# One fused layer kernel: the experts' results scattered to token order by GpSimd, and read back by plain transfers

## The reference

```
out = x + attention(xn) + experts(xn)
```

```
gate_logits = xn @ gate_w + gate_b                     # 8 experts
top_idx     = top_k(gate_logits, 2)
all_out     = relu(xn @ expert_w[e] + expert_b[e])     # e = 0..7
experts     = mean of all_out over the two chosen e
```

## Time and profile before

| | us |
|---|---|
| time, median of 3 runs | 1613.08 (1612.5 to 1616.36) |
| the profiled execution's own time | 1613.21 |
| its span | 1611.5 |
| TensorE busy | 1512.8 (94%) |
| VectorE busy | 1137.4 (71%) |
| ScalarE busy | 902.2 (56%) |
| GpSimd busy | 583.6 (36%) |
| mean granted clock of TensorE | 0.975 of full |

### The profile page before, as it was taken

How to read it: one execution, slowest core, us unless ns; L and a number is a source line. 1 busy time by engine, 2 the same in 40 slices (tenths; PEclk the granted TensorE clock), 3 DMA queues, 4 the chain that set the end, 5 groups by cost and what they waited for, 6 DMA issues and landing times.

```text
span 1611.5 us, 44000 instructions
## 1 busy us (share of the span) xinstructions
PE 1512.8 (94%) x12544; PEld 809.9 (50%) x12545; DVE 1137.4 (71%) x2384; ACT 902.2 (56%) x1629; POOL 583.6 (36%) x788
## 2 busy tenths in 40 slices
PE   5799989999999999999999999999999899999697
PEld 2788844444444444454444444444444455555233
DVE  5788778887777777777777777777777244444366
ACT  1677746666666666666666666666666433332000
POOL 2444402323454454432232223222322543332653
PEclk9899979999999999999999999999999999999798
DMA  6588851223222322233223322232232466554787
GB/s 161 164 268 271 236 151 52 72 67 93 71 69 62 90 77 70 64 83 84 70 63 81 85 70 63 81 86 70 63 78 63 135 207 217 177 174 142 253 280 250
DMA packets 161456, 198.05 MB, mean 123 GB/s; under 512 B 45792, under 2 KB 95072, under 8 KB 161024
## 3 DMA queue, kind: packets, MB, share of 16 engines
q1 hardware_dynamic: 125088, 117.11, 24.9%
q10 hardware_dynamic: 23328, 44.60, 9.4%
q0 software_dynamic: 12992, 35.77, 7.4%
HBM read 109.13 MB, written 63.12 MB: 107 GB/s over the span
## 4 chain that ended last, share of the span: by engine, by line
PE 79%; DVE 8%; issue 5%; DMA 3%; SPq 2%; ACT 1%; POOL 1%; DVEq 0%; ACTq 0%; POOLq 0%
PE PS L1328 29%; PE PS L1383 28%; PE PS L1433 12%; PE PS L1457 5%; DVE pm L1122 4%; PE PS L1415 2%; DMA arena<-in_x 1%; SPq L423 1%; DVE mx L1127 1%; SPq L415 1%; DVE mx L1126 1%; DVE arena L988 0%; PE PS L1274 0%; DMA q_pieces<-w_hi 0%; DMA arena<-in_Wuv 0%
## 5 line engine op out<-in xcount | busy, mean ns | idle before, releaser
L1122 DVE TENSOR_REDUCE pm<-PS 128x1 f32<-128x512 f32 (+3 forms) x1280 | 717.0, 602 | 200.3 <-PE PS L1328 185.3
L871 ACT ACTIVATE arena<-PS 128x512 f32<-128x512 f32 (+1 forms) x1152 | 613.5, 574 | 300.0 <-PE PS L1328 277.9
L1328 PE MATMUL PS<-arena 97*64 97x512 f16 (+7 forms) x5120 | 693.5, 353 | 26.6 <-DVE pm L1122 20.3
L1383 PE MATMUL PS<-arena 128*33 128x512 f32 (+3 forms) x2560 | 634.7, 531 | 1.9 <-POOL arena L649 1.9
L1328 PEld LDWEIGHTS PS<-arena 96*64 96x64 f16 (+1 forms) x5120 | 329.3, 110 | 416.3 <-DVE pm L1122 140.1
L649 POOL TENSOR_SCALAR_AFFINE_SELECT arena<-arena 128x256 f32<-128x256 f32 (+1 forms) x256 | 111.5, 436 | 546.7 <-ACT arena L871 545.6
L1383 PEld LDWEIGHTS PS<-arena 128*33 128x33 f32 x2560 | 159.4, 111 | 81.5 <-POOL arena L649 2.6
L1433 PE MATMUL PS<-w_hi,arena 128*128 x576 | 172.5, 381 | 0.7 <-issue 0.7
L890 ACT ACTIVATE arena<-PS 128x1024 f16<-128x1024 f32 x72 | 73.8, 1024 | 143.5 <-PE PS L1415 141.4
L1328 PE MATMUL PS<-later,deny 128*64 128x128 f16 x1024 | 145.4, 222 | 0.0
L1186 DVE SCALAR_TENSOR_TENSOR arena<-PS,eb_bc 128x512 f32<-128x512 f32 x72 | 49.8, 692 | 114.8 <-PE PS L1433 111.3
(11 more groups left out here) (174 smaller groups left out, 1296.8 us busy)
## 6 DMA issues: line engine op xcount, KB each, us to landing
expert_rows<-arena SPq DMA_DIRECT2D x72, 256.0 KB
comb_hl<-arena SPq DMA_DIRECT2D x256, 64.0 KB
arena<-q_pieces ACTq DMA_DIRECT2D x90, 128.0 KB
arena<-k_pieces ACTq DMA_DIRECT2D x90, 128.0 KB
v_rows<-w_lo SPq DMA_DIRECT2D x8, 1056.0 KB, 7.5
arena<-in_x SPq DMA_DIRECT2D x16, 512.0 KB, 5.7
xn_rows<-arena SPq DMA_DIRECT2D x16, 512.0 KB, 6.1
q_pieces<-w_hi SPq DMA_DIRECT2D x32, 256.0 KB, 5.3
```

What stands on the lines that cost most here:

```text
L871: a.activation(probs[kk % 4][:, a_ * CH:a_ * CH + w], PS[:, s2_bank(k, x), 0:w], ACT.Exp, scale=SCALE).then_inc(s["exp_done"], 1)
L1122: v.reduce_max(pm[:, c, r, p:p + 1], PS[:, S1_BANK[n], 0:w], AX).then_inc(s["s1_done"], 1)
L1328: last = t.matmul(PS[h:h + P // 2, bank, cols], lhsT[:, h:h + P // 2], rhs, start=start, stop=stop)
L1383: last = t.matmul(PS[rows_, 6 + c % 2, CH - wds[a]:CH], v_sb[pu % 2][:, j + a, :], probs[pk % 4][:, a * off:a * off + wds[a]], start=p_ in ...
```

## The change

Two places per token are made in the internal tensor `expert_rows`, at rows 2 x token and 2 x token + 1, and behind them one row of its own for each place of the list (for the padding). What is written to the list is now the row number (2 x token + choice); the list's initial content is the numbers of the padding rows. It is read back as `row_of`; two more routing steps on VectorE make the token numbers `ids` from it (a shift right by one, and a minimum that sends the padding to the last token), and the table `place` with its copy goes.

In the expert stage GpSimd gathers with a column of `ids` directly, without the copy, and from the sixth tile on issues behind each gather one scatter: the finished tile of six tiles back goes from `y_sb` to its rows with an indirect DMA. `y_sb` has four buffers instead of two. SyncE no longer stores these tiles; it only waits for some of them, where its other transfers stood between the stores. In the last stage ScalarE, once all scatters have landed and the expert matmuls are done, loads for each tile of tokens its 256 rows with one plain DMA (512 KB) into one buffer of the ring, with the same waits as the gathers had. The loops of the last stage are written out on SyncE, VectorE and TensorE, and those of GpSimd in the expert stage; VectorE's loop over expert tiles has four tiles per round instead of two.

```diff
-    y_dram = nc.dram_tensor("expert_rows", (PT * P, E), f32, kind="Internal").ap()
+    y_dram = nc.dram_tensor("expert_rows", (NT * P * TOP + P * PT, E), f32, kind="Internal").ap()
...
+        y_g = [w_hi[:, :, :].rearrange("p e f -> p (e f)").bitcast(f32)[:, q * TOP * E:(q + 1) * TOP * E] for q in range(OUT_RING)]
+        Y_RING = 4
+        y_sb += [tD(E) for _ in range(Y_RING - len(y_sb))]
...
-            def expert_rows(i):
-                for u in range(2):
-                    sp.wait_ge(s["y_done"], count(i * 2 + u + 1))
-                    sp.dma_start(y_dram[ds((i * 2 + u) * P, P), :], y_sb[u]).then_inc(s[f"y_st{u}"], 16)
+            def expert_row(n):
+                sp.wait_ge(s["y_done"], count(n + 1))
+                sp.sem_inc(s["step_at"], 1)
...
-            with sp.Fori(0, NT // OUT_RING - 1) as m:
+            for m in range(NT // OUT_RING - 1):
...
+            for k in range(TOP):
+                g.iota(row_id[:, k], [[TOP * P, NT]], base=k, channel_multiplier=TOP)
+            link(g.iota(no_row[:], [[1, PT]], base=NT * P * TOP, channel_multiplier=PT))
...
-                                     in_=token_id[:, i:i + 1], in_offset=None).then_inc(s["id_done"], 16)
+                                     in_=row_id[:, k, i:i + 1], in_offset=None).then_inc(s["id_done"], 16)
...
-            def gather(i, q):
-                n = i * AHEAD_G + q
+            def gather(n):
+                q = n % AHEAD_G
                 pool.wait_ge(s["gt_ps"], count(n - AHEAD_G + 1))
-                g.tensor_copy(cur_id[:, q:q + 1], ids[:, ds(n, 1)]).then_inc(s["cur_done"], 1)
-                pool.wait_ge(s["cur_done"], count(n + 1))
-                pool.sem_inc(s["step_at"], 1)
                 g.indirect_dma_start(out=x_g[q], out_offset=None, in_=xn_dram,
-                                     in_offset=bass.IndirectOffsetOnAxis(ap=cur_id[:, q:q + 1], axis=0)
+                                     in_offset=bass.IndirectOffsetOnAxis(ap=ids[:, n:n + 1], axis=0)
                                      ).then_inc(s[f"xg_in{q}"], 16)
+            def scatter(n):
+                q = n % Y_RING
+                pool.wait_ge(s["y_done"], count(n + 1))
+                g.indirect_dma_start(out=y_dram, out_offset=bass.IndirectOffsetOnAxis(ap=row_of[:, n:n + 1], axis=0),
+                                     in_=y_sb[q], in_offset=None).then_inc(s[f"y_st{q}"], 16)
...
-            for u in range(2):
-                pool.wait_ge(s[f"y_st{u}"], count(16 * PT // 2))
-            for n in range(NT):
-                q, at = n % OUT_RING, n // B + n % B * ST
-                if n >= OUT_RING:
-                    pool.wait_ge(s["acc_done"], count(n - OUT_RING + 1))
-                for k in range(TOP):
-                    g.indirect_dma_start(out=y_g[q][k], out_offset=None, in_=y_dram,
-                                         in_offset=bass.IndirectOffsetOnAxis(ap=place[:, k, at:at + 1], axis=0)
-                                         ).then_inc(s[f"yg_in{q}"], 16)
+            for n in range(AHEAD_G, PT):
+                gather(n)
+                if n >= SCATTER_LAG:
+                    scatter(n - SCATTER_LAG)
+                if n == 3 * AHEAD_G - 1:
+                    low_part(BH - 1)
+            for n in range(PT - SCATTER_LAG, PT):
+                scatter(n)
...
+            for q in range(Y_RING):
+                act.wait_ge(s[f"y_st{q}"], 16 * PT // Y_RING)
+            act.wait_ge(s["z_ps"], count(PT))
+            for n in range(NT):
+                q, at = n % OUT_RING, (n // B + n % B * ST) * P * TOP
+                if n >= OUT_RING:
+                    act.wait_ge(s["acc_done"], count(n - OUT_RING + 1))
+                act.dma_start(y_g[q].rearrange("p (k d) -> p k d", k=TOP),
+                              y_dram[at:at + TOP * P].rearrange("(p k) d -> p k d", k=TOP)).then_inc(s[f"yg_in{q}"], 16)
...
+                elif n == ROUTED:
+                    dve.wait_ge(s["ids_in"], 16)
+                    last = v.tensor_scalar(token_of[:], row_of[:].bitcast(i32), 1, None, ALU.arith_shift_right)
+                    last = v.tensor_scalar(ids[:], token_of[:], float(NT * P - 1), None, ALU.min)
...
-            with dve.Fori(0, NT // OUT_RING) as m:
-                for q in range(OUT_RING):
-                    sums(m, q)
+            for n in range(NT):
+                sums(n)
...
-            with pe.Fori(1, NT // OUT_RING) as m:
+            for m in range(1, NT // OUT_RING):
```

More of the change, by code:

```diff
@@ L198, in layer_kernel @@
                  for w in (w_hi, w_lo) for q in range(NE * KB * E // (2 * E))]
-        y_g, acc = [spare[TOP * q:TOP * (q + 1)] for q in range(OUT_RING)], spare[TOP * OUT_RING:TOP * OUT_RING + OUT_RING]
+        per_w = NE * KB * E // (2 * E)
+        assert per_w == TOP * OUT_RING
+        y_g = [w_hi[:, :, :].rearrange("p e f -> p (e f)").bitcast(f32)[:, q * TOP * E:(q + 1) * TOP * E] for q in range(OUT_RING)]
+        acc = spare[TOP * OUT_RING:TOP * OUT_RING + OUT_RING]
         x_g = [x_g0[:, :]] + x_ahead
+        Y_RING = 4
+        y_sb += [tD(E) for _ in range(Y_RING - len(y_sb))]
         PS = ctx.enter_context(nc.psum_tensor("PS", [P, 8, CH], f32))
@@ L230, in layer_kernel @@
         START = 4
[L231 removed]
+        FROM_ZERO = ["id_zero", "id_done", "ids_in", "xg_in0", "xg_in1", "xg_in2", "xg_in3",
+                     "y_st0", "y_st1", "y_st2", "y_st3"]
         def count(n):
@@ L708, in heads @@
                     if kk == NU + FIRST_ROWS and not more:
-                        pool.wait_ge(s["ids_in"], 16)
+                        pool.wait_ge(s["routed"], count(ROUTED + 2))
                         pool.wait_ge(s["stage_free"], count(BH))
-                        gather(0, 0)
+                        gather(0)
                     if ids_from is not None and kk in FREE and ids_from + FREE.index(kk) < TOP * NT:
@@ L722, in _ @@
             pool.wait_ge(s["id_done"], 16 * TOP * NT)
-            pool.dma_start(ids[:], id_dram.rearrange("(p t) o -> p (t o)", p=P)).then_inc(s["ids_in"], 16)
+            pool.dma_start(row_of[:], id_dram.rearrange("(p t) o -> p (t o)", p=P)).then_inc(s["ids_in"], 16)
             with pool.Fori(IDS_IN, BH // 2 - 1) as it:
@@ L726, in _ @@
             heads(BH // 2 - 1, False, SPAN, None)
-            for q in range(1, AHEAD_G):
-                gather(0, q)
+            for n in range(1, AHEAD_G):
+                gather(n)
             add_halves(BH - 1, 1)
[L731 to L737, removed]
-            for u in range(2):
-                pool.wait_ge(s[f"y_st{u}"], count(16 * PT // 2))
-            for n in range(NT):
-                q, at = n % OUT_RING, n // B + n % B * ST
-                if n >= OUT_RING:
-                    pool.wait_ge(s["acc_done"], count(n - OUT_RING + 1))
-                for k in range(TOP):
-                    g.indirect_dma_start(out=y_g[q][k], out_offset=None, in_=y_dram,
-                                         in_offset=bass.IndirectOffsetOnAxis(ap=place[:, k, at:at + 1], axis=0)
-                                         ).then_inc(s[f"yg_in{q}"], 16)
+            for n in range(AHEAD_G, PT):
+                gather(n)
+                if n >= SCATTER_LAG:
[4 more added lines that the diff above has]
+                scatter(n)
         @block.scalar
@@ L1176, in _ @@
                 heads(it, True, SPAN)
-            heads(BH // 2 - 1, False, SPAN)
-            dve.wait_ge(s["eb_done"], count(1))
[L1180 to L1191, removed]
@@ L1193, in _, with rows @@
-            for i in range(BESIDE):
-                rows(i)
-            scale(BH - 1, 1)
[L1196 to L1200, removed]
+            assert TOP == 2
+            for kk in SPAN:
+                heads(BH // 2 - 1, False, [kk])
+                if kk in (NU + 2, NU + 4):
+                    routing(ROUTED + (kk - NU) // 2 - 1)
+            dve.wait_ge(s["eb_done"], count(1))
+            def rows(i, q):
+                n, u = i * Y_RING + q, q % 2
+                e = dve.value_load(expert_of[0:1, ds(n, 1)], min_val=0, max_val=NE - 1)
+                dve.wait_ge(s["z_ps"], count(n + 1))
+                dve.wait_ge(s[f"y_st{q}"], i * 16)
+                v.scalar_tensor_tensor(out=y_sb[q], in0=PS[:, u, :], scalar=1.0 / (WS * TOP),
+                                       in1=eb_bc[:, ds(e, 1), :].rearrange("p e c -> p (e c)"),
+                                       op0=ALU.mult, op1=ALU.add).then_inc(s["half_done"], 1)
+                dve.wait_ge(s["half_done"], count(n + 1))
+                v.scalar_tensor_tensor(out=y_sb[q], in0=y_sb[q], scalar=0.0, in1=bo_bc[:],
+                                       op0=ALU.max, op1=ALU.add).then_inc(s["y_done"], 1)
@@ L1201, in sums @@
+            for n in range(2 * BESIDE):
+                rows(n // Y_RING, n % Y_RING)
+            scale(BH - 1, 1)
+            for n in range(2 * BESIDE, 2 * Y_RING):
+                rows(n // Y_RING, n % Y_RING)
```

(5 more changed lines are left out.)

39 lines of the change are left out of this document (16 added, 23 removed).

## The result

The changed kernel takes 1585.56 us (median of 4 runs, 1584.48 to 1586.56) against 1613.24 (4 runs) before, on the same chip: ratio 0.9823, 95% interval 0.9807 to 0.9838. The forecast was 1585. The span of the profiled execution is 1583.2 us.

The account below looks back on a forecast made before the run. Last stage taken as bound by DMA bytes once the crawl is gone, just behind TensorE: data from 1494.5 plus 84.3, 2.05 and 2.7 give span 1583.6, plus 1.7 outside makes 1585 us; range 1577 to 1604.

Parts of the forecast that it names:

- Bounds and floor: Last stage: 384 TensorE matmuls at 0.216 us take 83.0 us, so TensorE's floor of the whole span is 1576.3 us.
- DMA ends last: Last stage: 31.2 MB at 370 GB/s (341 to 391) take 84.3 us and end 7 us after TensorE's floor.
- Start: Hand-over: after the last expert sum at 1489.07, ScalarE issues its first load at 1493.4 and data flows from 1494.5.
- Expert stage at cost 0: Expert stage: GpSimd's gather and scatter take 2.55 of 3.037 us per tile, hidden under busy TensorE; 31 us if cover fails.
- the crawl moves into the expert stage: Rival, 8%: GpSimd's descriptor work starves engines during the experts, 61 us lost there less 28 gained, ending at 1646 us.
- the crawl: Last stage before: during GpSimd's gather runs, TensorE and other engines advance very slowly without data dependence; 28 us at stake.
- GpSimd becomes the pace: Rival, 7%: in the expert stage GpSimd needs 3.50 us per tile, giving 1616 us at worst, 1600 at the mean.
- Removed from the last stage: GpSimd's 80 us: Last stage: 64 indirect gathers at 1.25 us each leave GpSimd; 32 plain loads from ScalarE bring the same 16.78 MB.
- The crawl as a cause: Last stage: slow stretches accompany GpSimd's gather runs and go with them; rival that they stay: 15%, 1598 to 1613 us.

Follow-up runs that it names:

- Q: A second chip used for follow-up experiments; the unchanged kernel before took 1589.4 us there (13 runs).
- S: Another chip used for follow-up experiments; the unchanged kernel before took 1589.5 us there (8 runs).
- R: A chip used for follow-up experiments; the unchanged kernel before took 1609.4 us there (19 runs), the changed kernel 1581.76 us, ratio 0.9824.
- the first pair's chip: The chip, with no number on record, where the main result was measured: kernel before 1613.24 us, changed kernel 1585.56 us.

## Why the prediction was right, and where only its sum was

*Bounds and floor.* Right. 83.0 us forecast for TensorE, 83.04 measured; floor 1576.3, and with the 6.9 us of a later start 1583.2, which is the span. The sum of 1583.6 had DMA end the stage from a start on time; two terms were off and cancelled. That the time came within 1 us is luck.

*"DMA ends last", at 370 GB/s.* Mis-sized. From 1505 to 1560 the engines move 409 to 412 GB/s, above my upper end (391). Bytes do not end the stage: TensorE does. The term was 84.3 us from 1494.5, ending at 1578.8; TensorE's work ended at 1578.36, so the end was met by another engine from another start. That is not due to the late start: on Q and S, where the projection began at 1486.20 and 1486.94, it ran without a gap too, and the span ended 5.2 and 5.3 us behind it, against 4.8 here. The upper end came from dividing 403 GB/s by its share of 1.03, but shares of 1.03 and 1.04 lasted 55 us. Both ends were also read in stretches with gathers; on chip S, without the crawl, the gathering kernel moves 357 GB/s at a share of 1.00 and later 405 at 1.04.

*Start.* Last sum to ScalarE's first load: 1495.94 to 1499.77, 3.8 us, forecast 4.3. Its first data were used 3.55 us after that. Right, and it costs nothing, since eight tiles of projection lie ahead.

*Expert stage at cost 0.* This step failed: TensorE's stage is 5.4 us longer, 7.1 over the undisturbed 217.3, and the projection starts 6.9 us late. The prediction's own sign for wrong, expert tiles over 3.1 us apart, is there: 3.13 on the mean. Its accounting of GpSimd's time was right (0.98 and 0.99 per issue with 0.30 between, 2.57 per tile), and the cover that I named, TensorE's pace, held against that. What came instead was the rival "the crawl moves into the expert stage" in a mild form, about 7 us where I priced 61. My arguments against it were the DMA share of 0.59, the pause of 0.5 us per tile, and that no crawl began within 10 us of a pause. The stops came at a share of 0.57 and within 5 us of the start of a run of issues: GpSimd often makes four with 0.3 us between them and then stands still for about 1.2 us. TensorE never crawled as it did before. (The price of 1600 for "GpSimd becomes the pace" does not follow from its rows either: the mean of both durations is 3.02 us per tile, under the period.)

*Removed from the last stage: GpSimd's 80 us.* I gave this no price because the crawl took all the room. Without the crawl it is most of the gain, 10.4 of 11.6 us by the traces on S. The rule of the Trainium skill that I set beside the change ("DMA: Bandwidth & Descriptors", Issuing engines are not separate DMA queues: another issuer saves only issue time) describes that part. The trace on S agrees, with the addition that issue time was the pace: 1.33 us for 256 KB.

*The crawl as a cause.* That it goes with GpSimd's gathers: on R and the first pair's chip it is in all three traces with them, and in none of the three last stages without them, at a DMA share of 1.03. So full DMA engines alone do not make it, and written-out code does not cure it (it stays with the gathers on R); whether both edits are needed is open. That an unbroken run of GpSimd's issues is enough, as I held, is wrong as a general statement: on Q and S runs of up to 64 do nothing to TensorE. Something that differs between the chips or the runs on them is needed as well. Open: what that is, and whether on such a chip the issues alone or their bytes set it off. The experiments made for this ran on the others.

The time forecast hence holds for a chip with the crawl; on the others the same change is worth less than half of that. Of the gain of 28 us I put some 12 down to the pitch of the gathers, which is what the change brings where there is no crawl, and the other 16 to the crawl. That split is worked out, not measured: on a chip with the crawl the two were not taken apart. The times across chips agree with it: R costs the kernel before 20 us more than Q and S, and the changed kernel 4 to 5 us more than its version with loops there.

## What to carry to other kernels

An engine that only issues transfers can be the pace of a stage: before looking at bytes, compare what its issues take per tile (2.66 us here) with what the busy engine takes (2.59), and when each may begin. Moving the irregular access to the side where the producer is slow anyway (a scatter behind each expert tile) turned 64 gathers in the hurried stage into 32 plain loads. A stall that no dependence explains may belong to the chip: time the unchanged kernel on a second one before pricing its removal.

## What the runs showed of the hardware that was not expected

- One kernel takes 1586 to 1592 us on two chips and 1605 to 1616 us on another and on the first pair's chip, in over 50 runs. The one difference that I found in their profiles (Q has none of the kernel before) is a kind of stall: engines that advance by one instruction in about 0.7 us, or three engines released at one instant, while GpSimd issues indirect DMAs.
- Plain loads in 4 KB pieces beside stores and loads in 2 KB pieces held 409 to 412 GB/s for 55 us with TensorE at full clock.
- An indirect DMA of 128 rows costs GpSimd 0.95 to 1.0 us and a gap of 0.30 whether a row has 4 bytes or 2 KB. In the last stage of before none of the gathers went over 0.95 us except beside a TENSOR_TENSOR of VectorE, where they took 0.95 to 1.45.
- SyncE's plain stores took 0.34 us each from 1504 to 1520 in the changed kernel's last stage. After that, at a DMA share of 1.03, its plain DMA instructions took 0.34 to 4.07 us, many over 1.5: the queue's room is the likely reason, not shown. The longest, with the one before it:

```profile
1532.94 0.37 SPq L548 DMA_DIRECT2D out<-w_lo  x1
1533.36 4.07 SPq L542 DMA_DIRECT2D arena<-in_x  x1
```
